# Another order for all pieces of a two-layer transformer kernel: VectorE's SBUF passes against GpSimd's, and another opening

## What is computed

```python
def layer0(x, cond):                       # weights left out
    g1, g2, s1, s2, sh1, sh2 = split(silu(cond) @ ada_w.T + ada_b, 6)
    h = ln(x) * (1 + s1) + sh1
    q, k, v = split_heads(h @ qkv_w.T + qkv_b)
    o = softmax(rope(q) @ rope(k).T / 4) @ v
    x = x + (o @ proj_w.T + proj_b) * g1
    h2 = ln(x) * (1 + s2) + sh2
    return x + (gelu(h2 @ fc1_w.T + fc1_b) @ fc2_w.T + fc2_b) * g2
def layer1(x, cond):
    shift1, scale1, shift2, scale2 = split(swiglu(cond @ w_t1 + b_t1) @ w_t2 + b_t2, 4)
    h = rms(x, g1) * (1 + scale1) + shift1
    x = x + attention(h, rope) @ w_ao + b_ao
    h = rms(x, g2) * (1 + scale2) + shift2
    return x + swiglu(h @ w_fc + b_fc) @ w_fo + b_fo
```

## Time and profile before

| what | value |
|---|---|
| median of 3 runs | 814.12 us (813.14 to 817.34) |
| the profiled execution | 814.24 us |
| its span, first to last instruction | 812.4 us |
| mean granted TensorE clock | 0.962 |
| busy: PE, DVE, ACT, POOL | 741.3, 695.8, 449.2, 288.0 us |
| busy share: PE, DVE, ACT, POOL | 91%, 86%, 55%, 35% |

### The profile page before, as it was taken

The page is one execution under the profiler, slowest core; times in us unless marked ns, Lnnn a source line. Parts: engine busy times, 40 slices in busy tenths (PEclk is TensorE's granted clock), DMA queues, the critical chain, the costliest instruction groups (busy, mean ns, idle before and its releaser), DMA issues.

```text
span 812.4 us, 13189 instructions
## 1 busy us (share of the span) xinstructions
PE 741.3 (91%) x4576; PEld 452.9 (56%) x4576; DVE 695.8 (86%) x1177; ACT 449.2 (55%) x681; POOL 288.0 (35%) x267
## 2 busy tenths in 40 slices
PE   4989888999989989799988999899999999999697
PEld 4463234456545654366535655376746666567397
DVE  4578899999998998899999999989888999966555
ACT  1215564677647764477645766556545644564332
POOL 0411204345254245432453344412453223323154
PEclk9968898999999999899998999899999999999999
DMA  8280523521311232313113034413111122200001
GB/s 323 81 209 17 156 76 88 147 67 41 90 41 54 60 80 84 91 27 106 40 40 83 21 82 118 117 40 92 40 41 53 40 75 83 67 1 1 1 2 52
DMA packets 32882, 59.42 MB, mean 73 GB/s; under 512 B 7856, under 2 KB 12080, under 8 KB 32560
## 3 DMA queue, kind: packets, MB, share of 16 engines
q1 hardware_dynamic: 32816, 58.58, 25.1%
HBM read 39.42 MB, written 18.87 MB: 72 GB/s over the span
## 4 chain that ended last, share of the span: by engine, by line
PE 45%; DVE 33%; issue 10%; ACT 5%; DMA 3%; POOL 1%; SPq 1%; POOLq 0%; ACTq 0%; DVEq 0%
DVE top L1043 14%; PE ring L848 11%; PE ps_o L800 7%; PE ps_b L865 5%; PE ring L742 5%; PE ring L785 5%; PE ring L770 5%; DVE mlp L1131 4%; PE ring L755 3%; DMA mlp<-in_w_split 2%; ACT pr L1313 2%; DVE act_h L1145 2%; DVE xn L989 1%; DVE mlp L1152 1%; DVE xn L992 1%
## 5 line engine op out<-in xcount | busy, mean ns | idle before, releaser
L1043 DVE TENSOR_REDUCE top<-ring 128x2 fp32r<-128x1024 f32 x256 | 304.2, 1214 | 20.1 <-PE ring L785 19.1
L1313 ACT ACTIVATE pr<-ring 128x1024 f32<-128x1024 f32 x256 | 253.6, 1024 | 119.2 <-PE ring L770 105.9
L1447 POOL TENSOR_TENSOR act_l<-mlp,act_h 128x256 fp32r<-128x256 f32 x128 | 100.9, 788 | 254.3 <-DVE act_h L1145 254.3
L800 PE MATMUL ps_o<-pr,va 128*17 128x512 f32 x1024 | 134.8, 611 | 1.4 <-ACT pr L1313 1.2
L770 PE MATMUL ring<-qt,kt 49*128 49x512 f32 x512 | 112.9, 465 | 19.8 <-DVE top L1043 7.1
L785 PE MATMUL ring<-kt,qt 48*128 48x512 f32 x512 | 113.5, 469 | 11.3 <-DVE top L1043 5.7
L1327 ACT ACTIVATE mlp<-ring,col 128x256 f32<-128x256 f32 x128 | 60.8, 475 | 93.3 <-PE ring L848 70.7
L770 PEld LDWEIGHTS ring<-qt,kt 49*128 49x128 f32 x512 | 46.8, 186 | 103.8 <-issue 46.2
L785 PEld LDWEIGHTS ring<-kt,qt 48*128 48x128 f32 x512 | 47.9, 192 | 79.9 <-issue 26.3
L1131 DVE SCALAR_TENSOR_TENSOR mlp<-mlp 128x256 f32<-128x256 f32 x128 | 63.0, 492 | 26.7 <-ACT mlp L1334 24.9
L848 PE MATMUL ring<-hh,wl 128*128 128x256 f32 x384 | 82.8, 298 | 2.4 <-DVE top L1043 1.2
(11 more groups left out here) (83 smaller groups left out, 1018.3 us busy)
## 6 DMA issues: line engine op xcount, KB each, us to landing
scratch<-high SPq DMA_DIRECT2D x16, 512.0 KB, 3.9
scratch<-low SPq DMA_DIRECT2D x16, 512.0 KB, 4.3
qt<-scratch SPq DMA_DIRECT2D x64, 128.0 KB, 2.6
kt<-scratch SPq DMA_DIRECT2D x64, 128.0 KB, 2.7
mlp<-in_w_split SPq DMA_DIRECT2D x20, 256.0 KB, 3.2
qt<-scratch SPq DMA_DIRECT2D x64, 64.0 KB, 2.6
kt<-scratch SPq DMA_DIRECT2D x64, 64.0 KB, 2.7
xs<-in_x SPq DMA_DIRECT2D x4, 512.0 KB, 4.0
```

The lines of the kernel that those rows point to most:

```text
L800: last = nc.tensor.matmul(ps_o[32 * h:32 * h + HD + 1, :], va[:, u % 2, t, QUAD * g + h, :], pr[:, slot, :], start=(t == 0), stop=(t == T ...
L1043: nc.vector.tensor_reduce(top[:, n % 2, 0:4 * T].rearrange("p (e c) -> p e c", e=2)[:, :, c], pair[:, :, :], AX_X, ALU.max, negate=True).t ...
L1313: nc.scalar.activation(pr[:, at % NP:at % NP + 2, :], pair[:, :, :], ACT.Exp, scale=SCALE).then_inc(free, 1)
L1447: nc.gpsimd.tensor_tensor(act_l[:, at % 2, :], src, act_h[:, at % 2, :].bitcast(F32), ALU.subtract).then_inc(act_l_in, 1)
```

## The change

Only the numbers in `ORDER` are other numbers; every instruction is still there. The rows of the table tell a reader nothing by themselves; two of them:

```diff
-        ("act", "modulated"): (16, 17, 335, 336, 82, 83, 612, 613, 276, 277, 878, 879, 555, 556, 1157, 1158, 821, 823,
...
+        ("act", "modulated"): (12, 14, 333, 334, 95, 97, 613, 614, 272, 273, 873, 874, 551, 557, 1164, 1165, 828, 829,
...
-        ("dve", "norm_rows"): (10, 315, 40, 592, 265, 860, 551, 1140, 819, 1412, 1097, 1665, 1361, 1882, 1630, 2090,
...
+        ("dve", "norm_rows"): (10, 307, 79, 606, 262, 851, 550, 1144, 819, 1437, 1103, 1668, 1379, 1895, 1634, 2076,
```

More of the change, by code:

```diff
@@ L217 @@
 ORDER = {
[L218 to L226, removed]
@@ L238 @@
[L238 to L242, removed]
@@ L243 @@
-        ("pool", "low"): (79, 101, 133, 182, 281, 459, 604, 799, 892, 1034, 1172, 1359, 1462, 1571, 1659, 1787),
[5 rows of a table removed]
[L249 to L263, removed]
@@ L306 @@
-        ("dve", "lanes"): (150, 190, 225, 247, 321, 375, 481, 530, 600, 664, 755, 802, 875, 930, 1017, 1068, 1129,
-        1201, 1286, 1346, 1433, 1498, 1545, 1610, 1680, 1736, 1788, 1848, 1883, 1951, 2020, 2044),
-        ("dve", "output"): (153, 201, 230, 248, 344, 437, 516, 537, 628, 675, 757, 803, 911, 935, 1028, 1069, 1159,
-        1255, 1312, 1352, 1465, 1528, 1558, 1612, 1724, 1769, 1825, 1854, 1936, 1985, 2026, 2045),
-        ("dve", "back"): (222, 256, 461, 543, 690, 809, 953, 1079, 1260, 1355, 1539, 1619, 1804, 1856, 2015, 2046),
@@ L311 @@
-        ("pe", "project"): (260, 261, 262, 267, 547, 548, 553, 554, 815, 816, 822, 824, 1094, 1102, 1103, 1104, 1362,
-        1368, 1369, 1378, 1634, 1635, 1646, 1647, 1861, 1863, 1866, 1868, 2055, 2056, 2059, 2060),
-        ("dve", "residual"): (263, 268, 450, 549, 558, 559, 726, 817, 829, 830, 995, 1091, 1101, 1105, 1279, 1363,
-        1376, 1377, 1552, 1639, 1640, 1641, 1796, 1855, 1862, 1867, 1986, 2048, 2050, 2074, 2151, 2167),
-        ("pool", "residual"): (238, 239, 452, 535, 536, 540, 826, 851, 852, 873, 1133, 1135, 1136, 1137, 1303, 1417,
@@ L316 @@
-        1418, 1419, 1617, 1626, 1627, 1629, 1795, 1908, 1911, 1912, 2073, 2133),
-        ("dve", "split_h"): (339, 341, 616, 617, 883, 887, 1165, 1170, 1452, 1456, 1700, 1703, 1889, 1893, 2096, 2097,
-        2109, 2110),
-        ("pool", "split_h"): (323, 330, 607, 608, 922, 925, 1191, 1219, 1486, 1487, 1660, 1662, 1915, 1916, 2057,
[8 rows of a table removed]
-        ("act", "hidden"): (351, 352, 361, 364, 389, 390, 409, 411, 432, 433, 455, 456, 483, 484, 502, 505, 626, 627,
[6 rows of a table removed]
-        ("dve", "cube"): (358, 368, 374, 378, 396, 397, 414, 418, 438, 439, 454, 465, 491, 492, 508, 509, 630, 642,
@@ L341 @@
-        985, 994, 1002, 1016, 1022, 1029, 1062, 1063, 1186, 1190, 1204, 1208, 1217, 1229, 1243, 1245, 1269, 1277,
-        1295, 1302, 1310, 1311, 1336, 1337),
-        ("dve", "hidden"): (366, 373, 384, 385, 399, 406, 420, 421, 448, 449, 479, 480, 496, 497, 524, 525, 635, 645,
[6 rows of a table removed]
-        ("pool", "hidden"): (388, 402, 403, 404, 408, 410, 416, 428, 430, 431, 472, 473, 474, 499, 500, 501, 699, 703,
[13 rows of a table removed]
-        ("pool", "bias"): (1751, 2006, 2062, 2108),
-        ("sp", "store"): (1978, 2094, 2153, 2154, 2155),
+        ("act", "silu"): (7,),
@@ new lines @@
+        ("dve", "half_gate"): (22,),
+        ("dve", "silu"): (6,),
+        ("pe", "mod_0"): (2, 40),
+        ("dve", "norm_stats"): (1, 283, 72, 575, 244, 836, 508, 1128, 763, 1407, 1081, 1645, 1346, 1877, 1523, 2063,
+        2071),
+        ("dve", "norm_var"): (8, 288, 74, 599, 258, 840, 541, 1129, 798, 1423, 1093, 1646, 1368, 1879, 1581, 2065,
+        2079),
+        ("pool", "root"): (0, 284, 54, 598, 235, 936, 540, 1068, 883, 1383, 1047, 1631, 1317, 1894, 1590, 1991, 1992),
+        ("dve", "mod_0"): (11, 69),
@@ new lines @@
+        ("dve", "norm_rows"): (10, 307, 79, 606, 262, 851, 550, 1144, 819, 1437, 1103, 1668, 1379, 1895, 1634, 2076,
+        2083),
+        ("pe", "norm_turn"): (3, 343, 102, 618, 267, 877, 560, 1166, 826, 1456, 1117, 1688, 1398, 1898, 1648, 2067,
+        2068),
+        ("act", "modulated"): (12, 14, 333, 334, 95, 97, 613, 614, 272, 273, 873, 874, 551, 557, 1164, 1165, 828, 829,
[3 rows of a table added]
+        ("act", "take"): (18, 28, 38, 56, 100, 116, 167, 168, 281, 282, 331, 332, 565, 566, 607, 608, 833, 838, 848,
@@ new lines @@
+        849, 1121, 1130, 1137, 1148, 1405, 1409, 1430, 1431, 1651, 1652, 1653, 1667),
+        ("dve", "cosine"): (17, 52, 122, 179, 295, 341, 584, 615, 850, 875, 1134, 1175, 1411, 1485, 1657, 1703),
+        ("pool", "sine"): (20, 47, 99, 192, 287, 312, 574, 624, 938, 939, 1085, 1090, 1359, 1425, 1658, 1659),
+        ("dve", "rotate"): (24, 58, 129, 181, 313, 370, 585, 645, 852, 882, 1154, 1186, 1441, 1546, 1671, 1709),
+        ("act", "high"): (30, 61, 140, 205, 326, 374, 594, 649, 859, 887, 1156, 1204, 1451, 1603, 1682, 1803),
@@ new lines @@
+        ("pool", "low"): (35, 50, 126, 208, 298, 400, 578, 728, 943, 954, 1125, 1199, 1417, 1545, 1661, 1746),
[5 rows of a table added]
+        ("dve", "take_v"): (25, 37, 49, 59, 120, 142, 144, 207, 296, 297, 314, 315, 567, 580, 590, 591, 858, 863, 868,
+        871, 1155, 1158, 1159, 1162, 1435, 1436, 1445, 1447, 1663, 1664, 1680, 1681),
+        ("dve", "widen"): (34, 57, 65, 70),
+        ("pe", "gates"): (45, 51, 55, 64),
+        ("dve", "gates"): (62, 66, 77, 78),
+        ("pe", "net_1"): (19,),
+        ("dve", "net_1"): (33,),
@@ new lines @@
+        ("act", "net_gate"): (44,),
+        ("dve", "net_gate"): (41,),
+        ("pe", "net_2"): (43, 46, 53, 63, 67, 73, 82, 83),
+        ("dve", "net_2"): (107,),
+        ("sp", "load"): (23, 13, 27, 16, 39, 9, 32, 68, 89, 309, 279, 88),
+        ("sp", "load_w"): (26, 85, 98, 104, 108, 160, 161, 196, 233, 318, 319, 372, 1289, 1290, 1306, 1314, 1315,
+        1328, 1338, 1345),
+        ("act", "split_w"): (29, 90, 123, 136, 137, 152, 153, 169, 174, 216, 217, 300, 1380, 1382, 1395, 1396, 1420,
@@ new lines @@
+        1422, 1426, 1438),
+        ("dve", "split_w"): (113, 115, 143, 145, 156, 163, 164, 188, 259, 336, 337, 338, 1400, 1401, 1402, 1410, 1416,
+        1421, 1432, 1470),
+        (None, "scores"): (110, 117, 124, 125, 131, 132, 138, 146, 150, 157, 158, 172, 176, 177, 183, 184, 187, 191,
[13 rows of a table added]
+        (None, "peaks"): (80, 81, 84, 87, 92, 93, 94, 96, 103, 105, 109, 111, 112, 118, 121, 128, 135, 147, 148, 151,
[13 rows of a table added]
+        ("dve", "top"): (101, 130, 178, 214, 241, 292, 357, 445, 519, 564, 633, 716, 783, 843, 896, 997, 1064, 1124,
[10 rows of a table added]
@@ new lines @@
+        ("dve", "lanes"): (155, 190, 229, 249, 321, 382, 472, 531, 600, 650, 741, 796, 857, 917, 1029, 1091, 1138,
+        1219, 1296, 1364, 1450, 1507, 1560, 1618, 1672, 1749, 1791, 1851, 1897, 1961, 2029, 2044),
+        ("dve", "output"): (159, 204, 231, 256, 347, 396, 480, 535, 602, 682, 787, 797, 860, 930, 1061, 1092, 1149,
+        1243, 1347, 1371, 1479, 1529, 1562, 1619, 1741, 1755, 1837, 1852, 1918, 1969, 2043, 2049),
+        ("dve", "back"): (212, 257, 476, 542, 735, 807, 993, 1098, 1252, 1375, 1542, 1625, 1764, 1855, 2026, 2051),
@@ new lines @@
+        ("pe", "project"): (263, 264, 265, 266, 554, 555, 556, 561, 816, 817, 821, 822, 1112, 1114, 1115, 1116, 1385,
+        1386, 1387, 1392, 1640, 1641, 1642, 1647, 1865, 1866, 1867, 1868, 2059, 2062, 2064, 2066),
+        ("dve", "residual"): (269, 271, 446, 552, 558, 559, 725, 809, 823, 824, 999, 1105, 1108, 1118, 1280, 1373,
+        1388, 1397, 1564, 1636, 1637, 1639, 1793, 1861, 1863, 1864, 1981, 2054, 2055, 2070, 2132, 2165),
+        ("pool", "residual"): (268, 270, 503, 547, 548, 571, 907, 908, 909, 933, 1042, 1063, 1065, 1066, 1284, 1322,
@@ new lines @@
+        1326, 1336, 1606, 1628, 1629, 1630, 1889, 1890, 1891, 1892, 1949, 2111),
+        ("dve", "split_h"): (342, 348, 617, 619, 885, 886, 1168, 1169, 1467, 1468, 1696, 1697, 1900, 1904, 2082, 2087,
+        2096, 2097),
+        ("pool", "split_h"): (308, 310, 611, 612, 952, 953, 1142, 1143, 1428, 1429, 1699, 1700, 1905, 1906, 1997,
[8 rows of a table added]
+        ("act", "hidden"): (358, 359, 373, 377, 399, 401, 419, 421, 434, 452, 457, 477, 478, 498, 512, 513, 634, 635,
[6 rows of a table added]
+        ("dve", "cube"): (356, 360, 376, 381, 395, 403, 413, 414, 438, 450, 468, 484, 485, 496, 516, 518, 639, 640,
@@ new lines @@
+        648, 657, 676, 677, 692, 697, 713, 722, 729, 739, 758, 759, 780, 788, 895, 903, 911, 915, 926, 934, 965, 966,
+        992, 996, 1014, 1028, 1046, 1048, 1056, 1067, 1188, 1189, 1207, 1213, 1224, 1225, 1255, 1256, 1266, 1277,
+        1282, 1307, 1308, 1332, 1349, 1350),
+        ("act", "tanh"): (361, 367, 375, 387, 402, 404, 424, 426, 441, 462, 473, 479, 492, 504, 523, 524, 636, 642,
+        652, 662, 673, 688, 694, 712, 717, 718, 732, 746, 761, 765, 779, 800, 897, 898, 921, 922, 931, 932, 973, 974,
@@ new lines @@
+        989, 1006, 1019, 1032, 1040, 1041, 1070, 1080, 1183, 1190, 1211, 1218, 1230, 1231, 1247, 1248, 1269, 1279,
```

(5 more changed lines are left out.)

17 lines of the change are left out of this document (removed), and 154 rows, old and new, of the table ORDER.

## The result

The changed kernel takes 756.13 us (median of 4 runs, 755.4 to 756.6), the kernel before 813.63 us beside it: a ratio of 0.928, with a 95% interval from 0.925 to 0.931. That is 57.5 us, where the prediction had 19 and its range ended at 778. The profiled execution of the changed kernel took 755.99 us (span 754.2).

What follows compares the result with a forecast made beforehand. VectorE was taken to set the pace in layer 0, TensorE from 525 to 760 us. From 814.2 us, 6.5 for the opening and 12.5 for the moved passes gave 795.2, say 795, with a range of 778 to 814.

Steps and rivals of the forecast that it cites:

- What bounds the kernel: VectorE sets the pace from 160 to 525 us, busy 342.3 of 365; TensorE is the busier from 525 to 760.
- The opening, -6.5: Up to the first reduction: `modulated` ahead of the weight chunks brings that reduction from 52.62 to 46.1 us.
- The far bound: Opening: at most -9.1 us, with 2.5 us more gained if the first projection matmuls run at the later pace.
- The moved passes, -12.5: VectorE passes, mainly layer 0, moved out of GpSimd's way: 12.5 us saved, bounds 0 and -26.
- -11.5 - 2.9 + 1.9: Long passes on the chain save 11.5 us, layer-0 `hidden` casts at half 2.9; one new `split_w` collision costs 1.9.
- VectorE's busy time down by some 25 us: Sign over the whole kernel: VectorE's busy time falls by some 25 us from 695.8.
- The upper bound, -26: Moved passes: every long `norm_rows` row (20.1 us) and the casts' 5.9 us leave the time in full.
- everything pays: Rival, chance 0.10: 26 us of passes and 9.1 in the opening all count, giving 779 us.
- Layer 1 and the tail, nothing: Layer 1's MLP, where TensorE sets the stage, and the nearly unchanged tail were costed at nothing.
- Slower: Rival, chance 0.09: reductions come due before TensorE fills their PSUM pair; 36 more waits give 831 us.
- the other rivals: Only the opening pays (0.13, 807.7 us), only the passes pay (0.08, 801.7), both are given back (0.10, 814).

Runs made afterwards that it cites:

- e15: The changed kernel run once more, with nothing altered, for comparison on one chip: 755.74 us.
- e4: Pieces of the kernel before up to the first reduction, then the rest in the changed kernel's order: 765.14 us.
- e9: Changed kernel with only the three weight chunks back in their old place, ahead of the first `modulated`: 762.35 us.
- e7: Kernel before with only five `norm_rows` pieces moved ahead of the `residual` or `rotate` that sets GpSimd off: 800.19 us.
- e8: Kernel before with only GpSimd's subtraction for `hidden` cut to 16 columns: 794.75 us.
- e12: Kernel before with GpSimd's `residual`, `sine`, `low` and `split_h` cut to 16 columns, `hidden` at full width: 770.49 us.
- e1: Kernel before with all five large kinds of GpSimd work cut to 16 columns: 756.72 us.
- e11: Changed kernel with only four layer-1 `norm_rows` pieces put where GpSimd works: 766.85 us.

## Why the prediction was right in sign and wrong in size

- **What bounds the kernel**: right. VectorE sets the pace of layer 0, and the passes beside GpSimd are what it loses. The prediction read this from the earlier trace rows, and then did not use it in its sum.
- **The opening, -6.5**: about right. `modulated` comes at 12.26 us, projection at 14.03, as forecast, and the first reduction at 44.4 instead of 46.1 (in e15, the same kernel, at 42.2, so one trace settles it only within 2 us). By e4 and e9 the opening is worth 4 to 9 us at the end, but only in the new order; in the old one it is worth nothing. The far bound rested on a rule of the Trainium skill, page "TensorE: Matmul & The Clock Gate", section "What's actually happening". It was not reached: the first eight projection matmuls, started at 14.03, still took 6.55 us, and four later ones 1.96; in e15 they took 5.07. The clock's records begin only at 19.8 us, and at 16.1 in e15, so the reason is not seen.
- **The moved passes, -12.5**: this is the step that failed, by a factor of almost four. The runs give about 48 to 50 for it (57.5 less the 9.7 by which the orders differ with short GpSimd work, or the 50.0 from the first reduction on). It was built as "-11.5 - 2.9 + 1.9" from the passes that stand on the chain. For those the prices were good: by the rows, four of the pieces that e7 moved were worth 2.0 + 1.9 + 1.7 + 4.0, 9.6 us, and the fifth was not on the chain; e7 gave 12.9 (8 to 15). What was missing is everything else that GpSimd stretches: `split_w`, `hidden`'s first operation, `output` and `cosine`, 19.5 us of busy time, none of it counted as a net gain, and the casts at half. The chain is one path: on the page of before it gives VectorE 33% of the span and TensorE 45%. Yet VectorE's queue, in strict order and busy for 342 of 365 us, passed on 0.88 to 1.07 us for each microsecond taken from it (e7, e8, e12, e1), on the chain or not. Among its signs the prediction had VectorE's busy time down by some 25 us, twice what it let leave the time; it fell by 42.9. So both steps were too small, the stretch that goes and the share of it that counts.
- **The upper bound, -26**: wrong for the same reason. It took in `norm_rows` and the layer-0 casts alone, so the range could not reach the result. For `norm_rows` it was a little high: it sets mean lengths against 345 ns, which is the step from row to row. With short GpSimd work (e1) the mean lengths are 407 and 349 ns, and the two groups lose 12.1 and 6.0 us of busy time, 18.1 in place of 20.1. The rival "everything pays" had the right mechanism and 779 as its time.
- **Layer 1 and the tail, nothing**: wrong. The last stage is 9.3 us shorter, with 8.2 us less of VectorE, and e11 shows that a pass that stands late and beside GpSimd there can cost more than its own length (5.22 us instead of 1.36, and 7.5 us lost).
- **Slower, and the other rivals**: VectorE's wait on raw score products did not grow; from the first reduction to the end of layer 0 it fell from 12.4 to 7.6 us. Neither GpSimd nor reductions that come due too early took the gain back.

What was not foreseen is that layer 0's stage shrank by more than VectorE's busy time, 40.7 against 34.2 us. The windows of before around unit 3's rows show one place where more than the stretch was lost:

```profile
424.00:427.50 3.50, 1.62 (x9) 0.80 (x7) 3.50 (x4) 1.19 (x2) 3.06 (x2) 1.00 0.25 54
427.50:434.30 6.80, 4.28 (x12) 3.46 (x13) 5.85 (x9) 0.00 (x0) 1.66 (x1) 0.50 0.44 127
434.30:441.00 6.70, 6.70 (x49) 3.54 (x48) 5.98 (x10) 6.03 (x9) 2.57 (x2) 1.00 0.01 2
```

And TensorE's timeline there, in before:

```profile
422.97 1.99 PE L755 MATMUL ring<-wf,hf 128*128 128x256 f32 x8
...
430.02 3.78 PE L755 MATMUL ring<-wf,hf 128*128 128x256 f32 x8 [4.40 <-DVE va L1005]
```

The 5.36 us rows held up `take_v`, which TensorE waited for; it stood idle for 4.40 us, the granted clock fell to 0.50 (the 1.2 GHz level), and eight `v` matmuls took 3.78 us instead of 1.99. Beside unit 2's rows, 5.44 us from 328.14, TensorE is idle for 4.01 us too, and the clock is 0.50 from 332 to 338. After the change the rows take 1.4 us at both places, and the clock is 1.00 from 61 to 712 us. Over the span it went from 0.962 to 0.988. How the 6.5 us divide was not measured.
